# Wide ranks of the dilation in groups of 256 columns, with the counts of preceding groups added as offsets

## The reference, cut to what matters

```
row = carry[n]; num = sum(row)
sf = (num + 1) // 2 if num > 10 else 1
rank = cumsum(row)                       # running count along the row
rm = row & (rank % sf == 0) & valid      # at most a few entries of a row
carry[n] &= ~rm; carry[:, n] &= ~rm
```

## Time and profile before

| | us |
|---|---|
| median of 3 runs | 3010.84 |
| lowest, highest | 3008.50, 3018.25 |
| the profiled execution | 3018.62 |
| its span | 3016.8 |

### The profile page before, as it was taken

How to read it: one execution, slowest core, us unless ns; L and a number is a source line. 1 busy time by engine, 2 the same in 40 slices (tenths; PEclk the granted TensorE clock), 3 DMA queues, 4 the chain that set the end, 5 groups by cost and what they waited for, 6 DMA issues and landing times. The chain is left out here.

```text
span 3016.8 us, 41011 instructions
## 1 busy us (share of the span) xinstructions
PE 2784.0 (92%) x13446; PEld 1740.0 (58%) x13446; DVE 2277.1 (75%) x6124; ACT 1251.4 (41%) x3652; POOL 1082.2 (36%) x493
## 2 busy tenths in 40 slices
PE   6988999998999998899998997799999979999997
PEld 4655656655555655556655564455555545555786
DVE  4788998888988898898888886766566524676567
ACT  2544541545541554541554530233332224443564
POOL 4534333434333232321000000776666612443661
PEclk9999999999999999999999998899999989999998
DMA  6446336446327345326214102355554516996653
GB/s 215 134 136 206 105 99 213 137 130 210 109 84 227 113 133 192 105 62 190 91 57 164 60 15 98 128 212 215 191 188 181 189 70 242 396 395 270 241 200 126
DMA packets 304077, 492.27 MB, mean 163 GB/s; under 512 B 18544, under 2 KB 196080, under 8 KB 303856
## 3 DMA queue, kind: packets, MB, share of 16 engines
q1 hardware_dynamic: 303856, 489.57, 46.8%
HBM read 422.38 MB, written 67.11 MB: 162 GB/s over the span
## 5 line engine op out<-in xcount | busy, mean ns | idle before, releaser
L478 POOL TENSOR_SCALAR a_AT<-a_ats 128x512 uint8<-128x512 f32 x256 | 504.2, 1974 | 871.2 <-DMA a_ats<-in_adjT 809.3
L538 PE MATMUL a_acc<-a_ew,a_Hr 128*128 128x512 f32 x1536 | 796.0, 600 | 3.1 <-ACT a_hT L626 3.1
L717 DVE TENSOR_TENSOR a_ew<-adj,a_cos 128x512 f32<-128x512 f32 x768 | 522.6, 681 | 146.4 <-PE a_cos L531 145.2
L529 PE MATMUL a_cos<-a_nh 128*128 128x512 f32 x768 | 447.3, 582 | 2.4 <-DVE a_nl L709 2.4
L1286 POOL TENSOR_TENSOR b_dsum<-adj 128x1024 f32<-128x1024 f32 x16 | 141.9, 8870 | 662.2 <-DVE adj L1240 662.2
L538 PEld LDWEIGHTS a_acc<-a_ew,a_Hr 128*128 128x128 f32 x1536 | 292.3, 191 | 73.3 <-DVE a_ew L717 3.6
L640 ACT ACTIVATE a_vr<-a_D,a_sm_b,a_sm_sc 128x128 f16<-128x128 f32 x560 | 210.6, 456 | 246.0 <-DVE a_sm_b L766 245.4
L531 PE MATMUL a_cos<-a_nh,a_nl 128*128 128x512 f32 x768 | 306.3, 399 | 0.0
L530 PE MATMUL a_cos<-a_nl,a_nh 128*128 128x512 f32 x768 | 305.9, 398 | 0.0
L1130 PE MATMUL b_acc<-adj,b_h 128*128 128x512 f32 x512 | 224.3, 596 | 22.5 <-DVE adj L1240 22.5
L1290 POOL TENSOR_TENSOR b_dsum<-b_dsum,adj 128x1024 f32<-128x1024 f32 x96 | 225.8, 2352 | 14.1 <-POOL b_dsum L1290 0.5
(11 more groups left out here) (204 smaller groups left out, 4756.6 us busy)
## 6 DMA issues: line engine op xcount, KB each, us to landing
adj<-in_adjT SPq DMA_DIRECT2D x108, 1024.0 KB, 12.7
adj<-in_adjT SPq DMA_DIRECT2D x128, 512.0 KB, 5.8
a_ats<-in_adjT SPq DMA_DIRECT2D x256, 256.0 KB, 3.4
a_af<-in_adj SPq DMA_DIRECT2D x256, 256.0 KB, 3.4
scr_keep<-a_kp SPq DMA_DIRECT2D x128, 128.0 KB, 1.8
b_kp<-scr_keep SPq DMA_DIRECT2D x16, 1024.0 KB, 8.2
c_zi<-scr_z SPq DMA_DIRECT2D x32, 512.0 KB, 6.1
c_ai<-scr_ag SPq DMA_DIRECT2D x32, 512.0 KB, 7.0
```

Source lines behind the costliest of these rows:

```text
L478: e.tensor_scalar(AT[i][:, 4 * h:4 * h + 4, blk(k)].bitcast(U8), ats[h][:], 0.0, ONE8, ALU.is_gt, ALU.mult).then_inc(T["at"], 1)
L529: e.matmul(cos[j][:], n[:, blk(k)], n[:, half(j)], start=True, stop=False)
L538: e.matmul(acc[j][:], Hr[u % 2][:, k, :], ew[idx % 3][:], start=(k == 0), stop=(k == NK - 1)).then_inc(E["agg"], 1)
L717: e.tensor_tensor(ew[idx % 3][:], adj[g % 2][:, k, half(j)], cos[j][:], ALU.mult).then_inc(E["ew"], 1)
```

## The change

- PE: a block q of a half is multiplied only to the end of its own group of 256 columns: 256, 128, 256 and 128 columns in place of 512, 384, 256 and 128.
- PE: `first` multiplies by six columns in place of two. The four new columns hold, for group g, the doubled count of all blocks that lie before the group. The tables `two1` and `zero1` become one table `steps`.
- DVE: the copy of `base` takes six columns per graph. At the end of the `check` step come four small operations (three where k is 6 or 7), each behind a wait for the one before: the block's own last count, its addition to the groups after it, the product with the scale, the sum with the offset. The result is `wb`, one offset per graph and group.
- ACT: each half takes two instructions of 256 columns with offsets from `wb`, in place of one of 512. The one-column instruction for `b1` goes. The first of a block waits for `wb`.
- PE's waits: for i > 0 each half waits for `av` of the same half of graph i - 1; nothing waits for `b1`.

```diff
+        C["steps"] = sb("steps", [128, 2, NK, 6], BF16)
...
+            e.memset(C["steps"][:], 0.0)
...
+            e.memset(C["steps"][:, 1, :, 0], 2.0)
+            e.memset(C["steps"][:, :, :, 1], 1.0)
+            for g in range(1, 4):
+                e.memset(C["steps"][:, :, 0:2 * g, 2 + g], 2.0)
...
-                        e.matmul(rank(i)[:, 132:134], AT[i][:, q, blk(k)], (C["two1"] if q < k else C["zero1"])[:],
+                        e.matmul(rank(i)[:, 132:138], AT[i][:, q, blk(k)], C["steps"][:, 1 if q < k else 0, q, 0:6],
...
-                    elif j == 0:
-                        e.wait_ge(T["b1"], Q * n + i)
                     else:
-                        e.wait_ge(T["av"], 8 * n + 2 * i)
+                        e.wait_ge(T["av"], 8 * n + 2 * i - 1 + j)
...
-                        t = e.matmul(Dp[:, j, q * 128 - j * 512:512],
+                        odd, end = q % 2, (q // 2 + 1) * 256 - j * 512
+                        t = e.matmul(Dp[:, j, q * 128 - j * 512:end],
                                      Sd[i][K % 2][:] if q == k else AT[i][:, q, blk(k)],
-                                     C["UL"][:, 0:512 - (q * 128 - j * 512)], start=(q == 4 * j),
+                                     C["UL"][:, 0:128 if odd else 256], start=(q == 4 * j),
...
-                    e.activation(v[c % 3][:], Dp[:, j, :], ACT.Abs,
-                                 bias=b1[:, i:i + 1] if j else sm["b"][:, i:i + 1],
-                                 scale=sm["sc"][:, i:i + 1]).then_inc(T["av"], 1)
-                    if j == 0:
-                        if n:
-                            e.wait_ge(T["av"], 8 * (n - 1) + 2 * i + 2)
-                        e.activation(b1[:, i:i + 1], Dp[:, 0, 511:512], ACT.Identity, bias=sm["b"][:, i:i + 1],
-                                     scale=sm["sc"][:, i:i + 1]).then_inc(T["b1"], 1)
+                    if i == 0 and j == 0:
+                        e.wait_ge(T["wb"], 4 * (n + 1))
+                    for g in range(2):
+                        t = e.activation(v[c % 3][:, g * 256:g * 256 + 256], Dp[:, j, g * 256:g * 256 + 256], ACT.Abs,
+                                         bias=wb[:, i, 2 * j + g:2 * j + g + 1], scale=sm["sc"][:, i:i + 1])
+                    t.then_inc(T["av"], 1)
...
+                    flat_base = base[:].rearrange("p b i c -> p (b i) c")
+                    suffix, done = (n % NK) // 2 + 1, 4 * n + 2
+                    e.tensor_tensor(own[:], flat4, flat_base[:, :, 1], ALU.subtract).then_inc(T["wb"], 1)
+                    if suffix < 4:
+                        e.wait_ge(T["wb"], 4 * n + 1)
+                        e.scalar_tensor_tensor(flat_base[:, :, 2 + suffix:6], bc(own[:], 4 - suffix), 2.0,
+                                               flat_base[:, :, 2 + suffix:6], ALU.mult, ALU.add).then_inc(T["wb"], 1)
+                    else:
+                        done = 4 * n + 1
+                    e.wait_ge(T["wb"], done)
+                    e.tensor_tensor(wb[:], flat_base[:, :, 2:6], bc(sm["sc"][:], 4), ALU.mult).then_inc(
+                        T["wb"], 4 * n + 3 - done)
+                    e.wait_ge(T["wb"], 4 * n + 3)
+                    e.tensor_tensor(wb[:], wb[:], bc(sm["b"][:], 4), ALU.add).then_inc(T["wb"], 1)
```

More of the change, by code:

```diff
@@ L103, in build @@
         C["UL"] = sb("UL", [128, 512], BF16)
-        C["two1"] = sb("two1", [128, 2], BF16)
-        C["zero1"] = sb("zero1", [128, 2], BF16)
+        C["steps"] = sb("steps", [128, 2, NK, 6], BF16)
         C["eps"] = sb("eps", [128, 1])
@@ L169, in dve @@
             e.memset(C["flags"][:], 0.0)
-            e.memset(C["zero1"][:], 0.0)
-            e.memset(C["two1"][:], 2.0)
+            e.memset(C["steps"][:], 0.0)
             e.memset(C["U2"][:], 1.0)
@@ L177, in dve @@
             e.tensor_scalar(C["mv"][:], C["mf"][:], 0.0, None, ALU.not_equal)
-            e.memset(C["two1"][:, 1:2], 1.0)
-            e.memset(C["zero1"][:, 1:2], 1.0)
+            e.memset(C["steps"][:, 1, :, 0], 2.0)
+            e.memset(C["steps"][:, :, :, 1], 1.0)
+            for g in range(1, 4):
+                e.memset(C["steps"][:, :, 0:2 * g, 2 + g], 2.0)
             e.wait_ge(S["ident"], 1)
@@ L370, in layer0 @@
                    "bst bag lnsd lnrs lnr " + " ".join(f"adj{i}{k}" for i in range(2) for k in range(NK)))
-        T = P.sems("ats0 ats1 at af0 af1 af2 sign low au x ct ru vr sd v8 wd av b1 rw tr kp kps0 kps1")
+        T = P.sems("ats0 ats1 at af0 af1 af2 sign low au x ct ru vr sd v8 wd av wb rw tr kp kps0 kps1")
         W, rows = P.sb("W", [128, 3, 128]), P.sb("rows", [128, 3, 128])
@@ L396, in layer0 @@
         v8 = P.sb("v8", [128, 128], FP8)
-        base = P.sb("base", [128, 2, 2, 2])
+        base = P.sb("base", [128, 2, 2, 6])
+        wb, own = P.sb("wb", [128, Q, 4]), P.sb("own", [128, Q])
         cnt = P.sb("cnt", [128, 2, 2])
-        b1 = P.sb("b1", [128, Q])
         vr = P.sb("vr", [128, Q, 128], F16)
@@ L585, in pe @@
                             e.wait_ge(T["rw"], 64 * (quad + 1))
-                            e.wait_ge(T["b1"], Q * NK * (quad + 1))
                         else:
@@ L647, in act @@
                         e.wait_ge(T["rw"], c - 2)
-                    if j:
-                        e.wait_ge(T["b1"], Q * n + i + 1)
-                    e.activation(v[c % 3][:], Dp[:, j, :], ACT.Abs,
-                                 bias=b1[:, i:i + 1] if j else sm["b"][:, i:i + 1],
-                                 scale=sm["sc"][:, i:i + 1]).then_inc(T["av"], 1)
-                    if j == 0:
-                        if n:
-                            e.wait_ge(T["av"], 8 * (n - 1) + 2 * i + 2)
-                        e.activation(b1[:, i:i + 1], Dp[:, 0, 511:512], ACT.Identity, bias=sm["b"][:, i:i + 1],
-                                     scale=sm["sc"][:, i:i + 1]).then_inc(T["b1"], 1)
+                    if i == 0 and j == 0:
[4 more added lines that the diff above has]
+                    t.then_inc(T["av"], 1)
         def dve(e):
@@ L748, in dve @@
                             e.wait_ge(T["rw"], 8 * n)
-                        e.tensor_copy(base[:], Dv[:, :, :, 132:134]).then_inc(T["ru"], 1)
+                        e.tensor_copy(base[:], Dv[:, :, :, 132:138]).then_inc(T["ru"], 1)
                         t0 += 1
@@ L916, in pe @@
                     for q in others:
-                        e.matmul(Dp[:, 0, 132:134], AT[:, q, blk(k)], (C["two1"] if q < k else C["zero1"])[:],
+                        e.matmul(Dp[:, 0, 132:134], AT[:, q, blk(k)], C["steps"][:, 1 if q < k else 0, q, 0:2],
                                  start=(q == others[0]), stop=(q == others[-1]))
```

## The result

| | us | ratio to the kernel before (95% interval) |
|---|---|---|
| before, four runs | 3010.76 (3008.50 to 3018.25) | |
| changed, four runs | 3037.15 (3025.68 to 3040.47) | 1.0077 (1.0045 to 1.0108) |
| changed, six runs in a second comparison | 3032.81 | 1.0069 (1.0053 to 1.0085) |
| changed, five runs in a third | 3034.86 | 1.0060 (1.0047 to 1.0073) |

The kernel became slower, by 0.6 to 0.8%. The kernel before had medians of 3012.41 us in the second comparison and 3016.55 us in the third. The forecast was no change, 3010 us, with a range up to 3034; the median of the first four runs is 3037. The profiled execution took 3025.68 us, the fastest of them.

The account below looks back on a forecast made before the run. PE (92% busy to 1790 us) was taken to bound the kernel, with DVE close behind (85%). Terms -54.6 + 47.1 + 6.8 = -0.7 us gave about 3010 us, no change; range 2974 to 3034 us.

Parts of the forecast that it names:

- the formula: PE, second wide stage: stall = (check's end + 0.70 or 0.51 + 1.98) - (stage's start - 0.11), if positive; sum 47.1 us.
- The ScalarE estimate for pieces of 256 columns: ACT, wide stages: straight line between 128 and 512 columns; four pieces take 1.94 us, as much as today, so no cost.
- the start after the first product: ACT, block 10: first half starts 3.44 us after the block's first product, waiting for DVE's new operations; today 0.74.
- The last rival: PE, wide stages: short products cost 98 ns each, saving only 31.6 us; +22 us, about 3033 us; chance 0.06.
- short products, two ScalarE pieces: PE and ACT, wide stages: fewer columns save 0.43 us in each of 128 stages, 54.6 us; split ACT costs nothing.
- VectorE's four operations: DVE, end of `check`: 22.8 us of added work lies in its waits for `cos`, so it costs nothing.
- the wait for the offsets: ACT waits for DVE's new operations, and PE's second-graph products for ACT: stalls of 47.1 us over 32 blocks.
- the clock: PE: four blocks with a first gap over 2 us lose 1.7 us each, 6.8 us; bounds 0 and 15 us.
- The wait weighs more than the saving: Second-graph products on PE: stalls 47.1, clock loss 15.3, DVE operations 11.4 against -54.6; +19 us, about 3030 us; chance 0.20.
- My threshold: PE, per block: the wait outweighs the saving once mean stall plus clock loss passes 1.71 us; forecast had 1.68.
- The saving comes through: PE, rounds and starts: half the stalls only replace later waits for DVE; -31 us, about 2980 us; chance 0.31.

Follow-up runs that it names:

- without offsets: Changed kernel without the four small DVE operations and ScalarE's wait for them, so group offsets are left out of the result: 2979.22 us, 0.9893 of the kernel before.
- operations unread: Changed kernel with the four DVE operations kept in place, but nothing reads their result and ScalarE does not wait for it: 2986.63 us, ratio 0.9914.
- short products alone: Kernel before with only the products shortened to the end of their 256-column group, counts of earlier groups left out: 2980.00 us, ratio 0.9890.
- long products: Changed kernel with the long products of the kernel before; offsets, waits and two ScalarE pieces stay: 3052.47 us, ratio 1.0120 to the kernel before.
- before, with a wait: Kernel before with one wait added: ScalarE's first wide instruction of a block waits for the block's four checks on VectorE: 3031.59 us, ratio 1.0060.
- operations before the checks: Changed kernel with the four DVE operations moved ahead of the block's checks: 2998.80 us, 0.9950 of the kernel before.
- operations after the last drops: Changed kernel with the four DVE operations moved right behind the last round's comparisons: 2989.93 us, 0.9921 of the kernel before.
- The fillings of 13 gaps: Changed kernel with unused products (106 in all) put ahead of PE's wait for `a_v` at 13 stages: 3024.34 us, 1.0033 of the kernel before.

## Why the prediction was wrong, point by point

**The mechanism was right.** "The products of the second graph, on PE, wait for the first graph's halves to be read, with all of PE's queue behind them" is what the waits show, in 28 blocks, as many as the formula gave a stall. The ScalarE estimate for pieces of 256 columns (0.56 us long, 1.94 us for four) was measured at 0.568 and 1.93 us, and the start after the first product was 0.1 us off. The last rival, products at 98 ns each, falls: a stage's products take 0.63 us.

**The steps that failed are terms of the sum.** Forecast and measured, against the kernel before:

| term | forecast | measured | by |
|---|---|---|---|
| short products, two ScalarE pieces | -54.6 | -40.1 | rest, kernel without offsets |
| VectorE's four operations | 0 | +9.1 | rest, operations unread less without offsets |
| the wait for the offsets | +47.1 | +35.3 | rest, changed less operations unread |
| the clock | +6.8 | +16.6 and +14.8 | clock's loss of the changed kernel |
| sum | -0.7 | +20.9 and +18.3 | mean times |

The first three measured terms are from the second comparison. The saving was put too large by 14.5 us and the wait by 11.8 us. These two errors nearly cancel, and that is luck. What moved the result is, in the main, the other two: the operations, which the sum took at nothing, and the clock.

*The operations.* The prediction hid all of their 22.8 us in VectorE's waits for `cos`; alone they cost 9.1 us of rest. Its own rival had reckoned with 11.4 us.

*The clock.* It was put at 6.8 us, for four gaps over 2 us, with a bound of 15. That gaps under 2 us are free was read from one gap of 1.74 us, in block 21. The same trace has another in block 22, and there the clock does fall; its mean over the 10 us from 1277 us on is 0.83:

```profile
1277.00 0.72 PE L575 MATMUL a_D<-UL,a_AT 128*128 128x512 bf16 x4 [1.75 <-ACT a_b L656]
```

Of the five gaps of 1.7 to 2.0 us that PE has in layer 0 of the kernel before, two are followed by the 1.2 GHz level, at the latest 3 us after they end; in the changed kernel's three profiles it is 12 of 21, and of the gaps over 2.0 us 31 of 46. And gaps were left out: those of blocks 2, 15, 21 and 22 behind `a_b`, at the fourth stage, were 1.74 us and became 2.2 us, which the formula for the second stage doesn't cover.

*The saving.* The prediction gave PE's columns as time, with 0 to 3 us set aside for ScalarE's slack. Of the 54.6 us the short products alone took 50.5 off PE's queue, and 11.7 us came back as idle time of PE, for `a_b` and `a_v` (7.3) and for the cleaned blocks (4.1).

*The wait.* The formula for the second stage came near wherever it was tried, each time too high, by 0.6 to 7.5 us:

| PE's wait at the second stage, us | by the formula | in the profile |
|---|---|---|
| changed | 47.1 | 39.6, 43.2, 40.7 |
| long products | 29 | 27.4 |
| before, with a wait | 15.6 | 12.0 |
| operations before the checks | 13 | 12.4 |
| operations after the last drops | 6 | 3.4 |

PE's whole wait for `a_v`, 55.6 to 58.8 us, holds another 16 us at the third and fourth stage. They don't belong to the offsets: the kernel without any has them too (16.2 us). They are part of what the saving lost.

**The rivals.** "The wait weighs more than the saving", 3030 us, at 0.20, is what happened, and its prices for the clock (15.3 us) and the operations (11.4) were near what was measured. My threshold was 1.71 us a block, against which I had 1.68; the distance was smaller than the error of any term. That should have given this rival a chance near that of the forecast, and the range an end above 3034. "The saving comes through" needed PE or VectorE to catch up after a stall. The added wait in the kernel before shows that they do not: 16.9 us for 15.6.

## What to carry to other kernels

Before you shorten work on the engine that bounds, look at what the shorter work needs that the longer one didn't, and where its producer stands in its own queue: four operations of 0.7 us together cost 35 us of waiting behind the checks, and next to no waiting one step earlier, where some 10 us of rest were left, mostly their own time. Where one engine is busy for 92% and another for 85%, don't count a saving on the first in full: here 50.5 us came off its queue and 11.7 us came back as its idle time. And sum idle time on TensorE with what follows it: the longer waits of the changed kernel came with 15 to 17 us of lower clock.

## What the runs showed of the hardware

- Unused products made the kernel faster. The fillings of 13 gaps raised the mean granted clock from 0.970 to 0.976 and took 10.5 us off the median.
- Executions of the changed kernel differ by 7 to 15 us within one comparison, and their mean clock by 0.003 to 0.005; 0.004 is 12 us of a run of 3033. The two don't follow each other one to one.
- A gap on PE doesn't set the clock by its length alone: of two gaps of 1.74 and 1.75 us in the kernel before, one was followed by the 1.2 GHz level and one wasn't.
- A ScalarE instruction on PSUM takes 454, 568 and 777 ns at 128, 256 and 512 columns here, a straight line to within 7 ns, and the next can start about 0.1 us before its end. By these starts splitting one of 512 in two costs about 0.24 us of the queue, and the two splits of a stage what the dropped instruction of one column did (0.46).
